# One core: x stored ahead of the sums' loads in the front, and the second norm's first row, z and w2 reordered in the tail

## The reference, cut to what matters

```python
mod = (silu(c) @ wmod).reshape(4, 6, 1, 256)          # sa, ca, ga, sb, cb, gb; ga, gb kept at |.| >= 0.25
h = layernorm(x) * (1 + ca) + sa
xBC, z, A_log = split(h @ W_in.T)                     # 256 + 2*32*64, 256, 32 columns
xs, B, C = split(conv4(xBC) + conv_b)                 # per channel, causal
a = -softplus(A_log);  L = exp(segsum(a))
y = einsum(C, B, L, xs) + D * xs
x = x + ga * ((y * silu(z + z_bias)) @ W_out.T)
h = layernorm(x) * (1 + cb) + sb
x = x + gb * (fwht(silu(h @ W1.T) * (h @ W3.T)) @ W2.T)   # hidden 1024
```

## Time and profile before

| | us |
|---|---|
| median of 3 runs | 534.34 |
| profiled execution, its own time | 538.0 |
| its span in the trace | 535.8 |
| TensorE matmuls busy | 520.5 (97%) |
| VectorE busy | 451.6 (84%) |
| ScalarE busy | 367.1 (69%) |
| GpSimd busy | 240.0 (45%) |
| granted TensorE clock, mean | 0.987 of full |

### The profile page before, as it was taken

How to read it: one execution, slowest core, us unless ns; L and a number is a source line. 1 busy time by engine, 2 the same in 40 slices (tenths; PEclk the granted TensorE clock), 3 DMA queues, 4 the chain that set the end, 5 groups by cost and what they waited for, 6 DMA issues and landing times.

```text
span 535.8 us, 19307 instructions
## 1 busy us (share of the span) xinstructions
PE 520.5 (97%) x7188; PEld 429.9 (80%) x7188; DVE 451.6 (84%) x746; ACT 367.1 (69%) x988; POOL 240.0 (45%) x465
## 2 busy tenths in 40 slices
PE   6998999999999999999999999998999999999997
PEld 3666788888888888888888888876889889889886
DVE  6899699999999999999999999998666656656342
ACT  1777789899898998988899899887424224234240
POOL 6763237777776766776786474581000000000000
PEclk9899899999999999999999999999999999999999
DMA  7736153343333335332432535576430232100101
GB/s 248 299 111 214 49 144 102 98 130 112 109 108 102 125 100 180 128 102 84 142 93 84 152 89 163 146 219 193 125 95 25 80 81 77 40 0 2 40 0 40
DMA packets 50289, 59.40 MB, mean 111 GB/s; under 512 B 8004, under 2 KB 44740, under 8 KB 49864
## 3 DMA queue, kind: packets, MB, share of 16 engines
q1 hardware_dynamic: 50248, 58.88, 35.9%
HBM read 48.75 MB, written 9.05 MB: 108 GB/s over the span
## 4 chain that ended last, share of the span: by engine, by line
PE 87%; DVE 4%; DMA 4%; SPq 2%; issue 1%; POOL 1%; ACT 1%; DVEq 0%; ACTq 0%; POOLq 0%
PE ps L384 20%; PE ps L385 20%; PE ps L386 20%; PE ps L574 9%; PE ps L548 5%; PE ps L629 4%; PE ps L595 3%; PE ps L612 3%; PE ps L698 2%; DVE acc L1123 2%; DMA gates<-gate_rows 2%; DMA x_channels<-acc 1%; SPq L247 1%; PE ps L481 1%; DMA u_sb<-in_u 1%
## 5 line engine op out<-in xcount | busy, mean ns | idle before, releaser
L1212 DVE SCALAR_TENSOR_TENSOR acc<-ps,cw_dve,acc 128x511 f32<-128x511 f32 (+2 forms) x384 | 255.9, 738 | 6.2 <-ACT acc L863 5.9
L1512 POOL TENSOR_TENSOR sums<-sums,far_above 128x256 f32<-128x256 f32 x128 | 94.5, 742 | 112.5 <-DMA sums<-packed_sums 106.4
L898 ACT ACTIVATE decay<-sums,p_slot 128x128 f32<-128x128 f32 (+1 forms) x512 | 143.2, 363 | 1.2 <-ACT p_slot L975 0.7
L863 ACT ACTIVATE acc<-ps,cw_act 128x512 f32<-128x512 f32 x128 | 95.4, 769 | 18.7 <-PE ps L386 16.6
L384 PE MATMUL ps<-ht_hi,wg_hi 128*128 128x512 f32 x256 | 107.5, 420 | 0.1
L385 PE MATMUL ps<-ht_lo,wg_hi 128*128 128x512 f32 x256 | 101.9, 398 | 0.0
L386 PE MATMUL ps<-ht_hi,wg_lo 128*128 128x512 f32 x256 | 101.9, 398 | 0.0
L1039 ACT ACTIVATE silu_sb<-ps 128x512 f32<-128x512 f32 x32 | 19.2, 599 | 78.6 <-PE ps L386 78.6
L1438 POOL TENSOR_TENSOR rstd<-vareps,minus_half 128x4 f32<-128x4 f32 x8 | 8.4, 1047 | 121.9 <-DVE vareps L1093 119.6
L386 PEld LDWEIGHTS ps<-ht_hi,wg_lo 128*128 128x128 f32 x256 | 48.5, 189 | 11.6
L1350 DVE TENSOR_TENSOR hid<-ps,silu_sb 128x512 f32<-128x512 f32 x32 | 22.1, 691 | 42.0 <-ACT silu_sb L1039 41.8
(11 more groups left out here) (144 smaller groups left out, 917.6 us busy)
## 6 DMA issues: line engine op xcount, KB each, us to landing
sums<-packed_sums SPq DMA_DIRECT2D x256, 96.0 KB, 2.7
wg_raw<-in_w_bc SPq DMA_DIRECT2D x8, 512.0 KB
y_parts<-yt_sb SPq DMA_DIRECT2D x64, 64.0 KB, 2.1
stage<-y_parts SPq DMA_DIRECT2D x32, 128.0 KB, 2.9
u_sb<-in_u SPq DMA_DIRECT2D x4, 512.0 KB, 4.9
stage<-in_w SPq DMA_DIRECT2D x1, 2048.0 KB, 14.0
x_channels<-acc SPq DMA_DIRECT2D x8, 256.0 KB, 2.5
ee<-running_sums SPq DMA_DIRECT2D x8, 256.0 KB, 3.9
```

The source lines that it names most:

```text
L863: af(acc[:, b % 2, t, :], ps[:, PROJ_BANK[t], :], ACT.Identity, bias=cw_act[:, t, 1:2], scale=cw_act[:, t, 0:1]).then_inc(s[f"tap_a{t}"], 1)
L898: i = af(decay_f[:, m:m + P - NS * h], sums[:, j, own], ACT.Exp, scale=-1.0, bias=p_slot[:, b * CH + n, j:j + 1])
L1212: stt(a[:, d:], ps[:, PROJ_BANK[t], 0:L - d], cw_dve[:, t, TAPS - 1 - d:TAPS - d], a[:, d:], ALU.mult, ALU.add).then_inc(s[f"taps{t}"], 1)
L1512: gp.tensor_tensor(v, v, far, ALU.add).then_inc(s["masked"], 1)
```

## The change

SyncE: `store_x(2)` moves from behind the first sums' loads to ahead of them; `store_x(3)` goes to behind those loads, ahead of `swap_halves(0)`. In the last step `gate_loads` moves behind the fourth sums' load, and the 128 KB of gate row 0 get a load of their own, into `xn2[:, 0]`, ahead of the last group. ScalarE, TensorE and VectorE orders change around both places, and transforms 2 and 3 of w2 get PSUM banks of their own (7 and 3).

```diff
+W2_BANK = [4, 5, 7, 3]
@@ SyncE
                 sp.dma_start(packed[:, h, :, 0:NS], full[:, :, 1 - h, NS:P]).then_inc(s["st_sums"], 16)
+            store_x(2)
             sp.wait_ge(s["st_sums"], 64)
@@ step(last)
                     load(u2[:], u_b[0], "ld_res")
-                    gate_loads()
...
                 load_sum(g, b, 3)
+                if last:
+                    gate_loads()
@@
                 load_sum(0, 0, j, first=True)
+            store_x(3)
             swap_halves(0)
-            store_x(2)
-            store_x(3)
@@
                 group(g)
+            sp.wait_ge(s["st_gates"], 16)
+            load(xn2[:, 0, :], gates_d[0:1, 0:D].to_broadcast([P, D]), "ld_gate0")
@@ TensorE w2_transform, z_project, up
-                    pe.wait_ge(s["w2_split"], n - 1)
-                mm(ps[:, 4 + n % 2, :], hadamard, ...
+                    pe.wait_ge(s["mixed"], 2 * NG * B)
+                mm(ps[:, W2_BANK[n], :], hadamard, ...
@@
-                        pe.wait_ge(s["w2_split"], 4)
+                        pe.wait_ge(s["w2_split"], zt + 1)
@@
+                        if m == 1 and b == 0:
+                            pe.wait_ge(s["w2_split"], 4)
@@
             scores(last, B - 1)
+            z_project(1, 4)
+            inter(last, B - 1)
+            norm2_transposes(0, 0)
+            intra(last, B - 1)
             w2_transform(2)
             w2_transform(3)
-            norm2_transposes(0, 0)
-            inter(last, B - 1)
-            intra(last, B - 1)
-            z_project(1, 4)
@@ ScalarE, front
             decays(0, 0, 0, True)
+            x_evacuate(2, 0)
+            x_evacuate(2, 1)
             gate_size()
-            x_evacuate(2, 0)
-            last_tap(0, 1, 1)
-            x_evacuate(2, 1)
-            act.wait_ge(s["xn_done"], CH * B)
-            af(e_rows, sums_t[:], ACT.Exp, scale=-1.0).then_inc(s["e_rows"], 1)
             act.wait_ge(s["wz_split"], 2)
             act.wait_ge(s["st_sums"], 64)
             act.wait_ge(s["st_zero"], 1)
+            last_tap(0, 1, 1)
             b_evacuate(0, 0)
             x_evacuate(3, 0)
             x_evacuate(3, 1)
             b_evacuate(0, 1)
+            act.wait_ge(s["xn_done"], CH * B)
+            af(e_rows, sums_t[:], ACT.Exp, scale=-1.0).then_inc(s["e_rows"], 1)
@@ ScalarE, tail
-            w2_upper(2)
             y_evacuate(r, r % 2, r // 2)
             state_copies(last)
-            w2_upper(3)
             h2_parts(0)
             y_evacuate(last, last % 2, last // 2)
+            w2_upper(2)
+            w2_upper(3)
             silu_gate(1)
@@ VectorE
-                dve.wait_ge(s["ld_gates"], 16)
+                dve.wait_ge(s["ld_gates" if b else "ld_gate0"], 16)
+                gate_row = gates[:, b:b + 1, 0, :] if b else xn2[:, 0:1, :]
@@
             w2_lower(0)
             residual1(0, 0)
-            w2_lower(1)
             residual1(0, 1)
             statistics2(0)
-            w2_lower(2)
+            w2_lower(1)
             normalise2(0)
             mix_unit(last)
+            h2_low(0)
+            w2_lower(2)
             w2_lower(3)
-            h2_low(0)
```

More of the change, by code:

```diff
@@ L177, in adaln_ssm_ffn_kernel @@
         st_sums ld_d ld_wg ld_wz ld_zb ld_wo ld_w13 ld_w2 ld_res st_out c_exp_done c_one c_rec c_silu_done
-        mod_mm mod_ev gate_mm gate_abs gate_sign gate_ev st_gates ld_gates bnst bnag eps1 rs half_set xn_done
+        mod_mm mod_ev gate_mm gate_abs gate_sign gate_ev st_gates ld_gates ld_gate0 bnst bnag eps1 rs half_set xn_done
         lnT_mm h32_done hhi_done hlo_done wx_split wz_split xp_mm xtap xtaps0 xtaps1 xT_mm xtok_ev a_mm abs_done
@@ L640, in w2_transform @@
                 else:
-                    pe.wait_ge(s["w2_split"], n - 1)
-                mm(ps[:, 4 + n % 2, :], hadamard, stage[:, NM * D + n * BANK:NM * D + (n + 1) * BANK], start=True,
+                    pe.wait_ge(s["mixed"], 2 * NG * B)
+                mm(ps[:, W2_BANK[n], :], hadamard, stage[:, NM * D + n * BANK:NM * D + (n + 1) * BANK], start=True,
                    stop=True).then_inc(s["w2_mm"], 1)
@@ L922, in w2_upper @@
                 nc.scalar.copy(w2_hi[:, 2 * n:2 * n + 2, :].rearrange("p m d -> p (m d)"),
-                               ps[:, 4 + n % 2, :]).then_inc(s["w2_hi_done"], 1)
+                               ps[:, W2_BANK[n], :]).then_inc(s["w2_hi_done"], 1)
             def gate_size():
@@ L1219, in w2_lower @@
                 h = w2_hi[:, 2 * n:2 * n + 2, :].rearrange("p m d -> p (m d)")
-                tt(w, ps[:, 4 + n % 2, :], h.bitcast(F32), ALU.subtract).then_inc(s["w2_split"], 1)
+                tt(w, ps[:, W2_BANK[n], :], h.bitcast(F32), ALU.subtract).then_inc(s["w2_split"], 1)
             def y_scale(b, kt):
@@ L1309, in residual1 @@
                 tt(x, ps[:, bank + h, :].rearrange("p (c d) -> p c d", c=2),
-                   gates[:, b:b + 1, 0, :].to_broadcast([P, 2, D]), ALU.mult).then_inc(s["res_mul"], 1)
+                   gate_row.to_broadcast([P, 2, D]), ALU.mult).then_inc(s["res_mul"], 1)
                 dve.wait_ge(s["ld_res"], (b + 1) * 16)
@@ L1362, in residual2 @@
                 dve.wait_ge(s["down_mm"], n + 1)
+                dve.wait_ge(s["ld_gates"], 16)
                 x = x_tok[:, n:n + 1, :]
```

## The result

The changed kernel takes 531.26 us (median of 5 runs, 530.18 to 531.44), the kernel before 534.63 in the same series (533.17 to 536.1): a ratio of 0.9922, 95% interval 0.9893 to 0.9952. A second series gave 530.62 against 534.12, ratio 0.9930 (0.9905 to 0.9956). The forecast was 527.7, a ratio of 0.9876. The direction held. Of the range, 526.0 to 531.0, only the upper end was reached: the ratio on the 534.34 shown gives 530.2, and the median itself lies 0.26 above the 531.0. The gain is 3.4 us by the medians and 4.2 by the ratio, not 6.65.

The account below looks back on a forecast made before the run. TensorE, busy 97%, was taken to bound the kernel, with time to gain in front and tail: 3.7 + 2.95 = 6.65 us, 538.0 to 531.35 profiled, 527.7 from the 534.34 median; range 526.0 to 531.0.

Parts of the forecast that it names:

- The two places: TensorE's idling and halved clock: front wait of 2.29 us for x's copy, tail wait of 2.53 us for the second norm.
- rival A: VectorE's waits stay or are replaced, holding TensorE to VectorE's 2.35 us lead; total gain 5.3, 529.0 us; chance 0.15.
- Front, SyncE and ScalarE: Front: x's stores issue earlier, ScalarE copies x before the last tap, x's transposes need no wait; front gain 3.7 us.
- first six taps: Front, VectorE: six taps of 0.66 us from 56.7 end at 60.0; TensorE wants them at 59.35, so waits 0.65.
- the same gain from it gives 527.7: Sum: the profiled execution's 6.65 us gain carried over to the shown median of 534.34, giving 527.7 us.
- seven matmuls x 0.20 and part of two more: Front, TensorE: with no long idle time ahead the clock stays up, saving 1.4 to 1.8 us, taken 1.75.
- rival B: Clock falls behind the new waits, 1.75 us in the front, about 1 in the tail; gain 3.9, 530.4 us; chance 0.09.
- The rule weighed: Clock changes depend on a fixed chip cadence and vary between runs, so the fall could return behind waits of 0.65 and 0.75.
- Tail: Last step: z of batch 1 fills TensorE's norm wait, up(0) starts 3.25 us earlier, 0.3 given back; gain 2.95 us.
- the residual's start: Tail, VectorE: gate row 0's own load and no w2_lower between halves let the norm's statistics start 0.95 us earlier.
- rival C: One place gives nothing: x's store lands late or z delays the norm's transposes; gain about 3, 531.3 us; chance 0.09.
- Rival D: Slower: swapped halves queue behind x's stores, GpSimd delays TensorE's first states; 536.3 us if landing takes 16.5; chance 0.04.

Follow-up runs that it names:

- e1: The kernel before, unchanged, run again for 12 more executions: median 534.29 us, ratio 1.0006.
- e7: Kernel before with only gate row 0's own load and all gates' load moved behind the fourth sums' load: ratio 0.9997.
- e4: Kernel before with only the change's tail: gate row 0's own load, gates' load behind the sums, orders of z, w2 and norm: ratio 0.9956.
- e8: Kernel before with only the tail's orders on TensorE, ScalarE and VectorE and the banks, one load of all gates as before: ratio 0.9953.
- e3: Kernel before with only the change's front: SyncE's order of x's stores and ScalarE's order: ratio 0.9981.
- e9: The changed kernel, unchanged, run again beside its variants: 530.62 us, ratio 0.9930.
- e5: Kernel before with only ScalarE's front order changed, SyncE as before: ratio 0.9986.
- e10: Changed kernel without SyncE's new order of x's stores, gate row 0's own load and the gates' load move: 531.38 us, ratio 0.9948.
- e6: Kernel before with only SyncE's order of x's stores changed, ScalarE as before: ratio 0.9994.
- e12: Kernel before with x of batch 3 stored later, behind the next weights' load and second swap: 540.42 us, ratio 1.0106.

## Why the prediction was right and wrong

**What bounds the kernel.** The two places were right, and the loop kept the lead entirely (B to C is 288.9 to 289.4 in all fourteen profiles). The worry that VectorE would hold it, rival A, is refuted in its effect. Of VectorE's 1.7 us of waits from 60 us on, which the prediction had go altogether, 0.9 remain, so they went by half.

**Front, SyncE and ScalarE.** Loads were forecast 0.55 late and hidden: 39.59 against 39.84, behind a start of the trace that was 0.80 earlier, so 0.55 late, hidden. Ahead of the tap the three operations, the store landing before it, x's transposes without a wait: all as walked. Between the two profiles A to B shrank by 3.79 for 3.7, and that closeness is in part luck. From A to the start of proj(0,1,0) it is 4.90 instead of 7.45, 2.55 for 2.6. From there to B it took 8.16 with the fall, 6.63 in e1 without, and 6.92 in the changed kernel, 0.22 of it the wait for VectorE: the fall costs 1.5 and not 1.75, the new wait 0.22 and not 0.65, and the two misses cancel. proj(0,1,0) on TensorE, in before, in e1 and after:

```profile
55.55 0.47 PE L384 MATMUL ps<-ht_hi,wg_hi 128*128 128x512 f32 x1
...
53.31 0.48 PE L384 MATMUL ps<-ht_hi,wg_hi 128*128 128x512 f32 x1
...
52.20 0.47 PE L388 MATMUL ps<-ht_hi,wg_hi 128*128 128x512 f32 x1
```

The prediction's "first six taps" that end at 60.0 are five: the sixth, tile 1's first, stands ahead of tile 0's start, and 60.0 - 56.7 is five times 0.66.

**The step that failed** is a sentence of the sum: "the same gain from it gives 527.7". In it two terms of the front were taken as the kernel's own that belonged to that one execution; by the mean clock, 5 of before's 100 are like it: the wait of 2.29 with the store's 2.17 ahead of it, and "seven matmuls x 0.20 and part of two more", 1.75. In the five profiles with before's front untouched the same stretch took 15.61 and 15.70 (before, e7), 12.86 (e4, the store 4.1 us and the wait 1.08) and 12.53 twice (e1, e8), and the change makes it 11.82. Against 12.53 that is 0.7 us, or 1.0 by the times of e3, instead of 3.7; how often the long wait comes isn't known better than by the clocks. The profile was of an execution of 538.0, 3.7 us above its kernel's median, and I wrote that difference down and carried the gain over unchanged. An execution that lies above the median for a cause of its own can hold waits that the median doesn't have; what removes them is worth that only there.

That 530.2 lies in the range is luck as well: it is outside the forecast's own 526.6 to 528.8, and the range reached so far up for rivals A and B, neither of which happened as told.

The rule weighed bears on this step, and I drew only half of it. The Trainium skill (TensorE: Matmul & The Clock Gate, Part 1: The HAM clock gate) says of a kernel's start that how many matmuls run at the lower clock differs between runs of the same kernel. I asked whether falls could come back in the changed kernel (rival B: they did not, the waits of 0.62 and 0.82 left the clock at 1.00), and not whether those of before were there in every run. The traces agree, and show it in the middle of a kernel too: a wait of 2.43 without a fall (e1), one of 1.88 with it (e7).

**Tail.** Sized well. xn2 at the forecast 0.95 earlier, the mix within 0.1, the transposes and intra 0.2 late, up(0) at 9.50 from the scores where 9.5 was walked. The fall behind the norm's wait is there in six of seven profiles, so its part of the gain is real. Given back were not 0.3 but 0.67: up(0) to the end is 157.4 in every profile with the new tail and 156.8 with the old. All of it lies ahead of out_project(1): 8.90 from up(0)'s start instead of 8.20, the wait of 0.25 for the first hidden tile and the slower restarts of two runs of matmuls. Another 0.3 goes to the last step's wait for VectorE, 0.82 for 0.50. That wait is 0.80 with the tail alone (e4) and 0.93 in e9, and 0.50 to 0.72 in the other profiles, those with a changed front (e3, e5) among them; why is open. 3.28 - 0.67 - 0.31 = 2.3, and 2.35 was measured with the tail alone (e4).

Wrong in its reason was the residual's start as a cause: with the orders alone (e8) the tail gives the same. The margin of 0.1 between z's end and xn2, which I named under rival C, was used up: the transposes' matmuls follow inter without idle time, and their weight loads waited 0.20 us for xn2, here as in e8 and e10. TensorE and the norm arrive together, and which of them sets the start isn't shown. The statistics start 0.55 us after D with the own row and without it (e8): with it, the residual's second half waits 0.24 us for out_project, which takes up the lead. D to up(0) is 0.7 longer without the own row in the one profile where the gates landed late (e10), and as short in the other (e8).

**Rival D**: GpSimd waited 4.2 us for the swapped halves instead of 2.5, and masked and scaled by 52.5; the states at 56.6 did not wait. As bounded.

## What to carry to other kernels

A profile is one execution: before its waits become terms of a sum, compare its time with the median, and if it lies well above it, take the gain of a wait that ends with a transfer, and of a fall of the clock, only as often as it occurs; more profiles of the same kernel begin to tell how often. Here the reordering that puts independent matmuls into a wait (z into the norm's) was worth nearly its walked size; the one that makes a transfer earlier took away a wait that only some executions have, and no time can be told from it. When a wait is filled, look at what the filling pushed behind it: here 0.67 us came back in the next stage.

## What the runs showed of the hardware

The slowest of x's stores, at the same place of SyncE's order, landed in 3.6 us in one execution (e1), in 4.1 in another (e4) and in 5.3 in two (before, e7), and TensorE's front wait was 0.75, 1.08 and 2.3 to 2.4 with it. And the clock does not follow the length of a wait alone: TensorE idled 2.43 us with no fall behind it (e1), 1.88 with one (e7), and 2.5 to 3.1 with one (before, e3, e5, e6, e12). Of before's 100 executions, those at a mean clock of 0.989 and 0.990 took 1.3 us more than those at 0.997, by the medians.
